# A two-layer decoder on one Trainium2 core: 310 products that nobody reads, on TensorE between stages and in first tiles

## What is computed

```python
x = x + L0_attn(_layernorm(x), ...)            # self-attention, 16 heads of 16, biases
x = x + L0_xattn(_layernorm(x), ctx, mask...)  # cross-attention, same heads, own layer norm on its delta
x = x + L0_ffn(_layernorm(x), ...)             # 32 experts, top 4, fixed capacity, one shared expert
x = x + L1_attn(_layernorm(x), ...)            # causal self-attention
x = x + L1_xattn(_layernorm(x), ctx, ...)      # 16 query and 4 key heads of 128, RMS norm, rotation
x = x + L1_ffn(_layernorm(x), ...)             # 64 experts, top 8, one shared expert, dense
```

## Time and profile before

| | |
|---|---|
| median of 3 runs | 1099.77 us (1099.46 to 1103.67) |
| profiled execution | 1104.6 us |
| its span, first to last instruction | 1102.8 us |
| PE, DVE, ACT, POOL busy | 845.6, 722.0, 486.8, 384.1 us |
| granted TensorE clock, mean | 0.893 of full |

### The profile page before, as it was taken

How to read it: one execution, slowest core, us unless ns; L and a number is a source line. 1 busy time by engine, 2 the same in 40 slices (tenths; PEclk the granted TensorE clock), 3 DMA queues, 4 the chain that set the end, 5 groups by cost and what they waited for, 6 DMA issues and landing times. The chain is left out here.

```text
span 1102.8 us, 17200 instructions
## 1 busy us (share of the span) xinstructions
PE 845.6 (77%) x5527; PEld 555.5 (50%) x5534; DVE 722.0 (65%) x1519; ACT 486.8 (44%) x1241; POOL 384.1 (35%) x348
## 2 busy tenths in 40 slices
PE   3995884343877716886788899888747999999997
PEld 2774663221666514663466667666633444444443
DVE  2772795654899916864778887776264655665565
ACT  0762441311555414552456555555343445454543
POOL 1110475366455465331544444343011121212120
PEclk9995897556999958996899999999857999999999
DMA  9900000222788621100000000000015443434441
GB/s 319 400 1 1 1 2 3 61 79 88 245 280 270 221 69 46 40 1 0 1 1 1 1 0 0 0 1 1 1 46 135 113 130 103 133 103 130 112 107 39
DMA packets 49346, 90.64 MB, mean 82 GB/s; under 512 B 7046, under 2 KB 30089, under 8 KB 48778
## 3 DMA queue, kind: packets, MB, share of 16 engines
q1 hardware_dynamic: 46218, 81.63, 23.8%
q0 software_dynamic: 3072, 8.30, 2.4%
HBM read 67.71 MB, written 22.29 MB: 82 GB/s over the span
## 5 line engine op out<-in xcount | busy, mean ns | idle before, releaser
L1182 POOL TENSOR_TENSOR m1ws<-m1raw,m1ws 128x768 f16<-128x768 f32 x33 | 55.0, 1668 | 219.1 <-ACT m1raw L1185 219.1
L716 POOL TENSOR_TENSOR xqr<-xqr,xt 128x512 f32<-128x512 f32 x48 | 61.2, 1275 | 140.0 <-DVE xt L1052 140.0
L1492 DVE TENSOR_TENSOR m1sg<-m1sg,m1Wb 128x512 f32<-128x512 f32 x66 | 62.2, 943 | 62.5 <-ACT m1sg L1410 52.0
L1452 PE MATMUL m1pg<-m1hs,m1ws 128*128 128x512 f16 x396 | 97.5, 383 | 3.9 <-PEq L58 3.9
L1463 PE MATMUL m1py<-m1ap,m1ws 128*128 128x512 f16 x396 | 96.3, 379 | 1.4 <-DVE m1ap L1504 1.4
L1452 PE MATMUL m1pu<-m1hs,m1ws 128*128 128x512 f16 x396 | 96.8, 381 | 0.0
L1414 ACT ACTIVATE m1ap<-m1ac 128x512 f16<-128x512 f32 x66 | 41.6, 630 | 117.2 <-DVE m1ac L1498 117.2
L1504 DVE TENSOR_TENSOR m1ap<-m1ac,m1ap 128x512 f16<-128x512 f32 x66 | 45.7, 692 | 45.9 <-ACT m1ap L1414 45.9
L1452 PEld LDWEIGHTS m1pg<-m1hs,m1ws 128*128 128x128 f16 x396 | 38.9, 98 | 51.4 <-issue 5.4
L1463 PEld LDWEIGHTS m1py<-m1ap,m1ws 128*128 128x128 f16 x396 | 38.6, 98 | 48.6 <-DVE m1ap L1504 2.3
L1452 PEld LDWEIGHTS m1pu<-m1hs,m1ws 128*128 128x128 f16 x396 | 39.0, 98 | 47.5 <-issue 1.4
(11 more groups left out here) (315 smaller groups left out, 2056.5 us busy)
## 6 DMA issues: line engine op xcount, KB each, us to landing
m1Wb<-wt_dram SPq DMA_DIRECT2D x66, 256.0 KB, 3.9
m1raw<-in_m_w SPq DMA_DIRECT2D x33, 384.0 KB, 4.2
slots_in<-zeros SPq DMA_DIRECT2D x1, 8192.0 KB, 26.7
m0rg<-in_m_wgu SPq DMA_DIRECT2D x32, 256.0 KB, 3.7
m0xg<-slots_in SPq DMA_DIRECT2D x32, 256.0 KB, 3.7
slots_out<-m0yo SPq DMA_DIRECT2D x32, 256.0 KB, 2.8
m0rd<-in_m_wd SPq DMA_DIRECT2D x32, 128.0 KB, 3.1
xwo<-in_x_wo SPq DMA_DIRECT2D x1, 2048.0 KB, 18.6
```

The costliest lines, as they stand in the source:

```text
L716: pool.tensor_tensor(blk, blk, t2[:, k % 2, :, :], ALU.add).then_inc(add_ok, 1)
L1182: pool.tensor_tensor(ws[:, u, 1, :], raw[:, u, :], ws[:, u, 0, :], ALU.subtract).then_inc(prep_ok, 1)
L1452: ins = pe.matmul(bank[:, :], part(ws, u, sw, c, which), hs[:, sh, c, CH * q:CH * q + CH], start=(k == 0), stop=(k == 5))
L1492: dve.tensor_tensor(sg[:, q, :], sg[:, q, :], Wb[:, u, CH * q:CH * q + CH], ALU.mult).then_inc(sw_ok, 1)
```

## The change

A new function issues float32 products of the identity with itself into a PSUM bank that nobody reads before it is written anew:

```diff
+def keep_busy(pe, bank, ident, count):
+
+    for _ in range(count):
+        pe.matmul(bank[:, 0:P], ident[:, :], ident[:, :], start=True, stop=True)
```

```diff
@@ attention16, PE (three times: a0, c0, a1)
             pe.wait_ge(zeroed, 3)
             if causal:
                 pe.wait_ge(ready, 1)
+            keep_busy(pe, p_s[:, 0, :], ident, 30 if causal else 12)
             turn(0)
             qk(0)
             values(0)
+            keep_busy(pe, p_s[:, 0, :], ident, 10)
             turn(1)
             scores(0)
...
             turn_ctx(NT - 1)
             project(NT - 1)
+            keep_busy(pe, p_q, ident, 20)
@@ attention128, PE
             def early(n, u):
+                keep_busy(pe, p_s[0][:, 0, :], ident, 15)
                 turn_h(0, 0, 0, 0)
                 pe.wait_ge(t_out, 1)
                 for k in range(8):
+                    if k >= 2:
+                        keep_busy(pe, p_s[0][:, 0, :], ident, 6)
                     if k == 2:
                         turn_h(1, 1, 1, 1)
...
                 for quarter in range(4):
                     project(n, u, quarter)
+                keep_busy(pe, p_s[0][:, 0, :], ident, 25)
@@ moe_dense, end of the router's block, PE
+                    keep_busy(pe, p_t[0][:, 0, :], ident, 30)
@@ moe_slots, end of the experts' block, PE
                     down(E0 - 1, 1)
+                    keep_busy(pe, p_s[0], ident, 30)
```

## The result

The changed kernel takes 1126.3 us (median of 4 runs, 1125.13 to 1127.09), the kernel before 1101.15 us in the same comparison (4 runs). The ratio is 1.0225, 95% interval 1.0205 to 1.0244: 2.2% slower. The prediction was 1121 us, slower. The profiled execution has a span of 1125.3 us at a mean clock of 0.922, against 1102.8 at 0.893. The clock rose and the time rose with it.

A forecast was written before the change was run, and what follows sets the result against it. Half-clock PE work bounds what can be won, at most 39 us of 77.8, only where PE carries the chain. Terms sum to +21 us on the 1099.8 median, giving 1121 us; range 1105 to 1134, the prediction's own case 0.81.

The forecast's parts named there:

- The barrier, and its price: At block ends all engines must empty, so unread products delay the next block; 0.47 us each at half clock, 0.25 at full.
- Rival A: At block ends, the barrier isn't held by products nobody reads; 1106 us in all, chance 0.08.
- The bounds: Per product 0.225 us gives 3 us back at four bare ends; with clock-rise and gain variations, 1108 to 1134 us.
- Rival C: Everywhere, products of an identity don't raise the clock, so all run at 0.47 us; about +73, 1173 us; chance 0.04.
- Rival B: Clock holds into the routers, with PE on the chain throughout its 77.8 us; 1087 us, chance 0.07.
- Start of a0: 12 products make `turn(0)` 3.1 us late, about 2.0 come back, 10 later products cost about 1 more; sum +1.1 us.
- Start of c0: 12 products cost +0.4, the clock holds over the pause four times in five, gain -3.6; sum -3.2 us.
- a1: At its start, 30 products cost 0; gain in `qk(0)` and around `turn(1)` -2.7 us. Its end was a separate +5.75.
- First tile of `attention128`: 15 products at the start +1.55, six times 6 between fills +2.2, clock gain -2.3; sum +1.5 us.
- Costed at nothing: Both blocks of `moe_slots` 0 under POOL's scatters and fetches; experts of `moe_dense` gain nothing, DVE waits for `m1Wb`.

The follow-up runs named there:

- e1: Changed kernel without the product groups at the ends of a0, c0, a1, `attention128` and the router of `moe_dense`: 1105.5 us, ratio 1.0007 to the kernel before.
- e2: Kernel before with only the seven product groups at block ends, none at starts or in first tiles: 1126.7 us, ratio 1.0193.
- e10: Kernel before with one group only, 40 products instead of 20 at the end of a0: ratio 1.009, 9.9 us of 1100.
- e8: Kernel before plus 38 products ahead of the experts of `moe_slots` and 9 and 24 in the router of `moe_dense`: ratio 1.0002.
- e9: Kernel before with only the 30 products behind the last projection in the experts of `moe_slots`: ratio 1.0008.
- e3: Changed kernel plus 10 products in PE's pause between the second hidden and first down of the `moe_dense` experts: 1126.7 us, ratio 1.0197 to the kernel before.
- e4: Changed kernel without the 15 and six times 6 products in the first tile of `attention128`: 1125.8 us, ratio 1.017 to the kernel before.
- e7: Kernel before plus products in idle time of the first tiles, and 8 in the last tile of `attention128`: ratio 0.9943.
- e5: Kernel before plus products only in gaps where its timeline shows PE idle, none at any block end: 1087.5 us, ratio 0.9874.
- e6: Kernel before plus products in idle time of the last tiles of `attention16` only (9, and 2 or 6): ratio 0.9945.
- e11: e5 plus 6, 4 and 2 more products in the later pauses of the last tile of `attention128`: 1084.5 us, ratio 0.9861 to the kernel before.

## Why the prediction was right, step by step

**The barrier, and its price.** Rival A (the barrier doesn't wait for them) fell by the rows after: each bare end starts its next block 0.8 to 0.9 us after the last product. e1, e2 and e10 show it on the time. The five ends cost 4.99 + 0.78 + 4.76 + 5.10 + 5.44 = 21.1 us in the table's terms (5.10 is from the end of DVE's last add to the router's first norm), where the prediction had 24.25. The price was a little off: at full clock a product takes 0.23 us (6.86 / 30 at the end of the experts of `moe_slots` in e1), not 0.25. The bounds had 0.225. In a1 the 20 products took 5.45 us, not 6.2.

**The clock rises under identity products.** Rival C (it doesn't) fell: 40 records behind cold projections took 5.67 us in a0, not 9.

**Rival B** wanted the clock to hold into the routers. After, in the router of `moe_dense`, it is at half from 819.7 for 30.7 us. What a fast clock all through a router would be worth was not tried.

**Start of a0.** `turn(0)` came 2.9 us later after the first norm, as said (3.1). At most 0.4 came back, not 2.0: the clock was full in the first half of `qk(0)` (1.28 us) and fell again in the second (1.91). The step assumed an even chance for the whole. The other side is weak too: a0 took 85.63 us before, but 84.71 to 84.74 in e8, e9 and e10, where its instructions are the same, and by those nothing came back.

**Start of c0.** The prediction gave four chances in five that the clock holds over the pause. Here it was at half from 109.8, and `turn(0)` was 1.9 us late, not 0.4. In e3, with the same products and the same pause of 2.44 us, it held: the 24 records took 2.92 us and `turn(0)` was 0.3 us late. In e4 it fell again (4.53 us). So the term is a matter of chance from kernel to kernel, and the profile after shows the worse case. The gain behind it, about 4.0 us, was there. Net -2.1 for -3.2.

**a1.** -4.3 for -2.7, but most of this is not the change's. The stretch from `turn(0)` to `attention128` was 97.13 us before, but 94.43 in e9, 93.17 in e8 and 94.06 in e7, three kernels that leave that tail as it was; in e5 and e6, which fill it, 90.39 and 90.68. Where the clock falls in that tail changes from kernel to kernel, so one profile of before is a weak base for this term. In the table's stretch, 109.80 us before and 105.52 after, e8, e9 and e10, which change nothing in a1, took 105.77, 107.09 and 107.04. Against them the change won 0.3 to 1.6 us in a1, less than was forecast.

**First tile of `attention128`.** The products cost at most what was said (+0.5 to +1.5, against 1.5). The term missed that a1's end group brings 1.0 to 2.1 us into it (34.61 to 33.59 and 32.55, e2 and e4).

**Costed at nothing.** The group in the router of `moe_slots` cost nothing (the start of its experts is at +7.37 us, as its router's start is). The 2.4 us that came in its experts have no cause shown: e1 to e4 had 124.0 to 126.0 us there too, the eight kernels without the group 122.2 to 123.9; a part of it is the wait for the last stores (e9 above). The 1.24 us ahead of a0's first norm are no effect of the change: that norm waits for the weights, and began anywhere from 11.06 to 12.38 us in the ten kernels whose start is that of before. The experts of `moe_dense` were costed at nothing by the wait for `m1Wb`. That the wait would then stand behind products at full clock as a pause, and take the clock away, was missed: 1.3 to 1.6 us of the 2.0 (e3).

**The sum** of 21 against 22.5 us in the profiles and 25.2 in the medians is thus partly luck: ends 3.2 us too dear, gains 0.9 too small (3.3 predicted; 4.2 measured is the sum of the other rows apart from both `moe` stages and the weights, with 0.2 of the rest of `attention128`), and 5.7 us from three places that had no term (1.24 + 2.43 + 1.98). The 0.9 of gains is itself owed to the profile of before, which was slow in a1.

The prediction took the sentence of the Trainium skill, "TensorE: Matmul & The Clock Gate", Part 1, that warming costs under 1% of a typical span, for a bound of 11 us on what could be won. As a bound for this kernel, which falls to half clock many times, it is not borne out: e11 wins 16.0 us, 1.4% (1.2 to 1.6), and its products add work and remove none.

## What to carry to other kernels

Work that only keeps an engine busy is free in a gap that something else ends, and costs what sticks out ahead of a barrier: in the table 95 products at four bare ends cost 20.3 us and the tiles won 4.2, while the same idea inside the gaps wins 1.3 to 1.4%. Size each group by the idle time in the timeline, and look at the next pause of the tile too: in two profiles the half clock that one filled pause put off landed on denser work. Look for the wait that an engine runs into next when it is earlier and at full clock; a pause there can drop the clock again. And before a term of 2 or 3 us is called a gain, look at the same stretch in other kernels that leave it alone: here it moved by as much.

## What the runs showed that was not expected

- The granted clock fell at the end of an almost idle stretch and met the work behind it: PE was busy for 0.94 of the 3.41 us from 860.67 at a granted clock of 0.95, and for all of the next 3.41 us at 0.55.
- A pause of 2.4 us between dense groups can be enough to lose the clock for 3.4 us (c0 and the experts of `moe_dense` after), but need not be: ahead of c0 in e3 the clock held over the same 2.44 us. The pauses of 0.9 us at `attention128` and 0.8 us before `m1pg` were not enough.
- The last tile of `attention16` has two forms in the profiles, with the same instructions: in a0 the half clock begins at 84.9 and lasts until c0 (before), or begins at 87.6 and is over after 3.4 us (e2), with the last projection at 2.07 or 1.13 us. e3 shows the second form with the code of the kernel after: its a0 took 85.50 us, against 88.12 after.
